# Attention output of a fused decoder layer carried by DMA transfers in token order, with new step orders on every engine

## What is computed

```python
x = x + attn(layernorm(x), W_qkv, W_out)            # causal, 16 heads of 16
x = x + mlstm(layernorm(x), ctx, ctx, gates, gain)  # 8 heads of 32
x = x + moe(layernorm(x), router, up, down)         # 8 experts, top 2

# the end of attn:
out = einsum('bnqk,bnkh->bnqh', softmax(scores), v)
out = out.reshape(B, -1, S)
return einsum('bds,nhd->bsd', out, W_out)
```

## Time and profile before

| | us |
|---|---|
| median of 3 runs | 968.09 |
| lowest, highest | 965.02, 971.19 |
| the profiled execution | 962.93 |
| its span, first to last instruction | 961.2 |
| TensorE busy | 887.1 |
| VectorE, ScalarE, GpSimd busy | 586.2, 487.4, 496.3 |

### The profile page before, as it was taken

One profiled execution on the slowest core, in us unless ns is written; L12 is line 12 of the kernel. 1 busy time (PEld: TensorE's weight loads), 2 busy tenths in 40 slices (PEclk: granted clock), 3 DMA queues, 4 the chain that ended last, 5 costly groups with the idle time before them and its releaser, 6 DMA issues.

```text
span 961.2 us, 31757 instructions
## 1 busy us (share of the span) xinstructions
PE 887.1 (92%) x11966; PEld 653.0 (68%) x11966; DVE 586.2 (61%) x1292; ACT 487.4 (51%) x839; POOL 496.3 (52%) x705
## 2 busy tenths in 40 slices
PE   5999999999997689899998988999999999999995
PEld 3667667667665356565564776778888888878783
DVE  4856766766764456777777657455555555555552
ACT  3667677677666367566455542333333333333331
POOL 2556666566565333366666667534444434444432
PEclk9999999999999799999888899999999999999998
DMA  9222443443445654455453233433332333233322
GB/s 283 70 57 67 93 129 90 96 127 90 92 119 121 172 183 132 146 177 179 144 162 118 90 86 89 87 62 51 48 51 47 53 49 52 46 52 52 47 34 23
DMA packets 133197, 92.96 MB, mean 97 GB/s; under 512 B 75712, under 2 KB 114112, under 8 KB 132928
## 3 DMA queue, kind: packets, MB, share of 16 engines
q1 hardware_dynamic: 119760, 73.10, 28.2%
q0 software_dynamic: 13296, 17.83, 11.1%
HBM read 54.65 MB, written 37.32 MB: 96 GB/s over the span
## 4 chain that ended last, share of the span: by engine, by line
PE 80%; DVE 7%; ACT 5%; issue 3%; DMA 2%; SPq 2%; another core or an unknown queue 1%; POOL 0%; DVEq 0%; ACTq 0%; POOLq 0%
PE pair L933 19%; PE pair L949 12%; PE pair L951 6%; PE pair L634 5%; PE pair L671 5%; PE pair L657 4%; PE pair L811 3%; PE pair L607 3%; PE pair L684 2%; PE pair L825 2%; PE pair L829 2%; PE pair L861 2%; PE pair L900 2%; PE pair L786 1%; PE pair L837 1%
## 5 line engine op out<-in xcount | busy, mean ns | idle before, releaser
L933 PE MATMUL pair<-XTs,WU 128*128 128x128 bf16 x3408 | 283.9, 219 | 5.9 <-DVE XTs L1269 2.9
L933 PEld LDWEIGHTS pair<-XTs,WU 128*128 x3408 | 238.1, 98 | 71.7 <-issue 8.7
L1603 POOL DMA_INDIRECT out_d<-XB x71 | 116.1, 1635 | 207.4 <-DVE XB L1291 174.0
L949 PE MATMUL pair<-WD,Hh 128*128 x568 | 214.8, 379 | 1.3 <-issue 1.3
L1469 ACT ACTIVATE Hf<-pair 128x512 f32<-128x512 f32 x142 | 84.8, 597 | 219.5 <-PE pair L933 207.9
L1282 DVE CAST Hh<-Hf 128x512 bf16<-128x512 f32 x142 | 64.5, 454 | 172.1 <-ACT Hf L1469 166.9
L951 PE MATMUL pair<-WD,Hl 128*128 x568 | 154.7, 272 | 0.0
L1284 DVE TENSOR_TENSOR Hl<-Hf,Hh 128x512 bf16<-128x512 f32 x142 | 99.5, 701 | 4.9
L1514 POOL TENSOR_SCALAR_AFFINE_SELECT PT<-PT 128x512 f32<-128x512 f32 (+1 forms) x96 | 73.9, 787 | 44.2 <-ACT PT L1320 28.7
L1576 POOL DMA_INDIRECT xs_scr<-XB,WGf x64 | 66.9, 1045 | 31.7 <-issue 18.2
L1488 POOL TENSOR_TENSOR LS<-LS,mhalf 128x2 f32<-128x2 f32 x48 | 34.1, 711 | 94.6 <-DVE LS L976 93.9
(11 more groups left out here) (243 smaller groups left out, 1728.9 us busy)
## 6 DMA issues: line engine op xcount, KB each, us to landing
XB<-xs_scr SPq DMA_DIRECT2D x71, 130.0 KB
STG<-wup_in SPq DMA_DIRECT2D x32, 256.0 KB
q_scr<-SPL SPq DMA_DIRECT2D x16, 512.0 KB, 4.2
STG<-wdn_in SPq DMA_DIRECT2D x32, 256.0 KB
o_scr<-On SPq DMA_DIRECT2D x32, 128.0 KB, 4.2
Mm<-o_scr SPq DMA_DIRECT2D x16, 256.0 KB, 3.0
CnT<-ctxt_in SPq DMA_DIRECT2D x16, 256.0 KB, 4.0
CX<-ctx_in SPq DMA_DIRECT2D x16, 256.0 KB, 4.4
```

The lines of the kernel that those rows point to most:

```text
L933: t = e.matmul(upb(j, k)[:, 128 * (fm % 4):128 * (fm % 4) + 128], WU[:, bass.ds(reg[j] * 4096 + off, 128)], XTs[:, r, hx, dk, :], start=n ...
L949: e.matmul(yb[r][:, 0:512], Hh[:, r, hsl], WD[:, bass.ds(reg[i] * 4096 + 512 * fk, 512)], start=fk == 0, stop=False, skip_group_check=True)
L1603: e.indirect_dma_start(out=out, out_offset=bass.IndirectOffsetOnAxis(ap=XS[:, i % NX, 256:257].bitcast(I32), axis=0), in_=Yf[:, i % NY, :] ...
```

## The change

- A4, its PSUM pair, On, Mm and the transposes of Mm go. ScalarE's copy to OTs now permutes the order within each partition.
- Step OT (SP) moves the row of denominators of each group of heads to `dnc`, 32 by 4 partitions, and stores OTs into `o_scr` in four transfers with runs of 64 floats, in the order of the tokens. XA (SP) reads it back with tokens in partitions. RC (VectorE) computes reciprocals times wsq, as 128x32. WB (SP) stores them with four transfers to the new scratch `r_scr`, BC (SP) reads them back, each row 16 times over, as XR with two transfers. X1 (VectorE) multiplies XA by XR and adds the product to x.
- The heads of Q and K are placed in another order in the weights, and PV picks V's columns accordingly.
- A6s, A6n and A6c run for batch b-3 instead of b-4 in a round, the query transposes in AX for b-3, the gate sums in MG for b-4 instead of b-5. `attention_rest` holds fewer steps.
- `ROUND` and `ORDER` have new orders on every engine. In attention SP loads the odd weight chunk of a round first and the even one after BC. ScalarE does A6c ahead of QK's copies. In the mLSTM TensorE does PV of part 2 and B5 between D of part 1 and D of part 2, and PV of part 0 at the end of the round; the two splits of a round on GpSimd no longer stand next to each other.

```diff
 ROUND = {
-    "tensor": "AX:1 MG:1 S1:0:0 T0:1:0 PV:2 S1:0:1 QK:-1 T0:1:1 S0:0 VX:0 T2:1 GT:15 weights:1:2 A4:2",
-    "vector": "Gp:16 weights:-2:0 A6s:4 weights:-1:1 S1:0:1 S0:0 VX:0 A4:2 weights:1:2 MG:0 AX:0 S1:-1:0 Gs:15 A0s:-3",
-    "scalar": "PV:2 A0n:-2 QK:-1 T0:1:1 Gt:13 A6c:4 weights:-2:0 A6n:4 VX:0 T2:1 weights:-1:1 AX:0 GT:15 MG:0 T0:0:0",
-    "gpsimd": "weights:0:2 split:0 T0:1:0 T0:1:1 split:0 GT:15 T2:1 A6c:4 A0s:-3 A6s:3",
-    "sync": "GT:15 load:0 A4:3 AX:1 Go:16 queries:16 decays:16",
+    "tensor": "MG:1 S1:0:0 T0:1:0 PV:2 S1:0:1 QK:-1 T0:1:1 S0:0 VX:0 T2:1 GT:15 weights:1:2 AX:0",
+    "vector": "A0s:-2 X1:3 S1:0:1 weights:-2:0 Gp:16 A6s:3 weights:-1:1 S0:0 weights:1:2 RC:2 Gs:15 MG:0 AX:0 S1:-1:0",
+    "scalar": "PV:2 A0n:-2 weights:-2:0 Gt:13 A6c:3 QK:-1 T0:1:1 VX:0 weights:-1:1 A6n:3 T2:1 AX:0 GT:15 MG:0 T0:0:0",
+    "gpsimd": "split:0 T0:1:0 A6s:3 T0:1:1 GT:15 weights:0:2 A6c:3 split:0 T2:1 A0s:-3",
+    "sync": "load:0:1 GT:15 BC:3 queries:16 load:0:0 AX:1 Go:16 OT:2 decays:16 XA:2 WB:2",
 }
 
-LIMITS = {"S1": (0, B - 1), "T0": (0, B - 1), "PV": (0, B - 2), "A0s": (0, B - 1), "A0n": (0, B - 1), "QK": (0, B - 1), "A6s": (0, B - 4),
-          "A6n": (0, B - 4), "S0": (0, B - 1), "VX": (0, B), "T2": (0, B - 1), "A6c": (0, B - 4), "A4": (0, B - 2), "AX": (-2, B), "MG": (0, B)}
+LIMITS = {"S1": (0, B - 1), "T0": (0, B - 1), "PV": (0, B - 2), "A0s": (0, B - 1), "A0n": (0, B - 1), "QK": (0, B - 1), "A6s": (0, B - 3),
+          "A6n": (0, B - 3), "S0": (0, B - 1), "VX": (0, B - 1), "T2": (0, B - 1), "A6c": (0, B - 3), "X1": (0, B - 3), "OT": (0, B - 2), "XA": (0, B - 2),
+          "RC": (0, B - 2), "WB": (0, B - 2), "BC": (0, B - 2), "AX": (-2, B), "MG": (0, B)}
 
...
             if kind == "load":
                 if ok(b):
-                    yield kind, 2 * b, 0
-                    yield kind, 2 * b + 1, 0
+                    yield kind, 2 * b + u, 0
             elif kind == "split":
                 if ok(b):
                     yield kind, parts, 0
...
                 yield kind, b, u
     yield "GE", 0, 0
     yield "PV", B - 1, 0
-    yield "MG", B + 1, 0
-    yield "A4", B - 1, 0
+    yield "OT", B - 1, 0
     yield "contexts", 0, 0
+    yield "queries", 1, 0
+    yield "WB", B - 1, 0
+    yield "XA", B - 1, 0
     yield "decays", 1, 0
-    yield "queries", 1, 0
     yield "contexts", 1, 0
...
-    return {(0, 0): (("A6s", z - 2), ("Mm", z), ("X1", z - 1), ("A6n", z - 2), ("A6c", z - 2)),
-            (0, 1): (("A6s", z - 1), ("XQ", z - 2), ("A6n", z - 1), ("A6c", z - 1)), (0, 2): (("X1", z), ("A6s", z)),
-            (1, 0): (("GA", z - 2), ("A6n", z)), (1, 1): (("XQ", z - 1), ("A6c", z)), (2, 0): (("XQ", z),), (2, 1): (("GA", z - 1),),
-            (3, 0): (("GA", z), ("Gt", 1)), (3, 1): (("GT", 1),), (3, 2): (("Gs", 1),), (4, 2): (("GE", 1),), (5, 0): (("Gp", 1),),
-            (5, 1): (("Go", 1),)}
+    return {(0, 0): (("RC", z), ("GA", z - 2), ("A6c", z - 1), ("X1", z - 1), ("A6n", z - 1), ("A6s", z - 1),), (0, 1): (("XQ", z - 1),),
+            (0, 2): (("X1", z), ("A6s", z),), (1, 0): (("GA", z - 1), ("A6n", z),), (1, 1): (("XQ", z), ("A6c", z),),
+            (2, 0): (("Gt", 1), ("GA", z),), (2, 1): (("GT", 1),), (2, 2): (("Gs", 1),), (3, 2): (("GE", 1),), (4, 0): (("Gp", 1),),
+            (6, 2): (("Go", 1),)}
 
...
 
 ORDER = {
-    "tensor": "D:0:0 B6:4 R4:5 PV:1:1 S:0:0 rest:0:0 D:0:1 PV:1:2 rest:0:1 D:0:2 B5:3 S:0:1 PV:0:0 rest:0:2 B4:1 S:0:2",
-    "vector": "B4x:2 rest:0:0 S:0:0 R5:5 R6:5 rest:0:1 B5s:2 S:0:1 rest:0:2 R2:4 B4:1 first:14 R3:4 S:0:2 R1:3",
-    "scalar": "rest:0:2 split:0 B4p:2 D:0:0 B5n:3 split:0 rest:0:0 D:0:1 rest:0:1 split:0 R1:4 B3:1 B5:3 D:0:2",
-    "gpsimd": "B4p:2 rest:0:0 sc:0 R6:5 split:0 split:0 sc:0 rest:0:1 sc:0 split:0 rest:0:2 B5s:2",
-    "sync": "load:0 rest:0:2 B1:0:1 B1:-1:0 rest:0:0 B4o:2 rest:0:1 row:15",
+    "tensor": "D:0:0 B6:4 R4:5 PV:1:1 rest:0:0 S:0:0 D:0:1 rest:0:1 PV:1:2 B5:3 D:0:2 S:0:1 rest:0:2 B4:1 S:0:2 PV:0:0",
+    "vector": "R5:5 R6:5 B4x:2 rest:0:0 S:0:0 rest:0:1 B5s:2 S:0:1 R2:4 rest:0:2 B4:1 R3:4 first:14 S:0:2 R1:3",
+    "scalar": "split:0 rest:0:2 B4p:2 D:0:0 split:0 R1:4 B5n:3 rest:0:0 D:0:1 rest:0:1 B3:1 split:0 B5:3 D:0:2",
+    "gpsimd": "split:0 B4p:2 sc:0 R6:5 split:0 rest:0:0 rest:0:2 sc:0 sc:0 split:0 rest:0:1 B5s:2",
+    "sync": "rest:0:2 rest:0:0 load:0 B1:0:1 B1:-1:0 B4o:2 row:15 rest:0:1",
 }
 
...
+    rsc = nc.dram_tensor("r_scr", (B, 16 * D), F32, kind="Internal").ap()
     qsc = nc.dram_tensor("q_scr", (B, 128, 2048), BF, kind="Internal").ap()
...
-        wsq = sb("wsq", [128, 2, NH], F32, ca)
-        On = sb("On", [128, 2, NH, 16], F32, ca)
-        Mm = sb("Mm", [128, 2, 2, 256], F32, ca)
+        dnc = sb("dnc", [128, 32], F32, ca)
+        rc = sb("rc", [128, 32], F32, ca)
+        wsq = sb("wsq", [128, 32], F32, ca)
+        XA = sb("XA", [128, 2, 2, 256], F32, ca)
+        XR = sb("XR", [128, 2, 256], F32, ca)
         QN = sb("QN", [128, 2, 256], F32, ca)
         CnT = sb("CnT", [128, 2, 256], F32, ca)
...
                         for par in range(2):
                             for kt in range(2):
                                 for j in range(4):
-                                    c = 17 * (8 * a + 2 * j + par)
+                                    c = 17 * (4 * j + 2 * a + par)
                                     if kt == 0:
                                         pt = blk(3 * b + a).rearrange("p (j r c) -> p j r c", j=4, r=2)[:, j, par, :]
...
                 elif kind == "VX":
...
-                    if ok(b - 3):
-                        m = b - 3
-                        w.wait_ge(l_m[m % 2], 16 * (m // 2 + 1))
...
-                            for tt in range(2):
-                                t = e.transpose(ps[:, 1, 256 * tt + 128 * dk:256 * tt + 128 * dk + 128], Mm[:, m % 2, dk, 128 * tt:128 * tt + 128], idf)
-                        t.then_inc(mT.sem, 1)
-                elif kind == "A4":
-                    pair_free(w, "A4", b)
-                    ps = pair_of("A4", b)
-                    w.wait_ge(ot_.sem, ot_.at(b))
-                    for tt in range(2):
-                        for g in range(4):
-                            o = ps[:, tt, 256 * (g // 2):256 * (g // 2) + 256].rearrange("p (j r c) -> p j r c", j=4, r=2)[:, :, g % 2, :]
-                            t = e.transpose(o, OTs[:, g, 128 * tt:128 * tt + 128], idf)
-                    t.then_inc(oT.sem, 1)
                 elif kind == "AX":
                     pair_free(w, "AX", b)
                     ps = pair_of("AX", b)
-                    for x_, m, src in ((1, b - 4, QN), (0, b + 2, xn)):
+                    for x_, m, src in ((1, b - 3, QN), (0, b + 2, xn)):
...
-                    if ok(b - 5):
-                        tensor_gate_sums(e, w, b - 5, ps[:, 1, 0:32])
+                    if ok(b - 4):
+                        tensor_gate_sums(e, w, b - 4, ps[:, 1, 0:32])
...
+        def vector_denominators(e, w, b):
+            w.wait_ge(l_dc, 16 * (b + 1))
+            w.wait_ge(l_wb, 64 * b)
+            e.reciprocal(dnc[:, :], dnc[:, :]).then_inc(dvc.sem, dvc.up())
+            w.wait_ge(dvc.sem, dvc.n)
+            e.tensor_tensor(rc[:, :], dnc[:, :], wsq[:, :], ALU.mult).then_inc(rc_.sem, 1)
+
+        def vector_residual(e, w, b):
+            r = b % 2
+            w.wait_ge(l_xa[r], 16 * (b // 2 + 1))
+            w.wait_ge(l_bc, 32 * (b + 1))
+            e.tensor_tensor(XA[:, r, :, :], XA[:, r, :, :], XR[:, :, :], ALU.mult).then_inc(dvc.sem, dvc.up())
+            w.wait_ge(dvc.sem, dvc.n)
+            e.tensor_tensor(xb(b), XA[:, r, :, :], xb(b), ALU.add).then_inc(x1_.sem, 1)
...
-                elif kind == "VX" and ok(b - 3):
-                    m = b - 3
-                    w.wait_ge(mT.sem, mT.at(m))
-                    e.tensor_tensor(xb(m), pair_of("VX", b)[:, 1, :].rearrange("p (t c) -> p t c", t=2), xb(m), ALU.add).then_inc(x1_.sem, 1)
-                elif kind == "A4":
-                    bv = pair_of("A4", b)[:, :, :].rearrange("p t (n c) -> p t n c", c=32)
-                    w.wait_ge(oT.sem, oT.at(b))
-                    w.wait_ge(l_o, 32 * b)
-                    e.reciprocal(bv[:, :, :, 16], bv[:, :, :, 16]).then_inc(dvc.sem, dvc.up())
-                    w.wait_ge(dvc.sem, dvc.n)
-                    e.tensor_tensor(rc[:, :, :], bv[:, :, :, 16], wsq[:, :, :], ALU.mult).then_inc(dvc.sem, dvc.up())
-                    w.wait_ge(dvc.sem, dvc.n)
-                    e.tensor_tensor(On[:, :, :, :].rearrange("p t n c -> p (t n) c"), bv[:, :, :, 0:16].rearrange("p t n c -> p (t n) c"),
-                                    rc[:, :, :].rearrange("p t (n a) -> p (t n) a", a=1).broadcast_to([128, 2 * NH, 16]),
-                                    ALU.mult).then_inc(on_.sem, 1)
+                elif kind == "RC":
+                    vector_denominators(e, w, b)
+                elif kind == "X1":
+                    vector_residual(e, w, b)
```

(54 more changed lines are left out.)

79 lines of the change are left out of this document (32 added, 47 removed).

## The result

The kernel after takes 963.03 us (median of 20 runs, 957.46 to 975.17); the kernel before, in as many runs beside it, 969.08 us. The ratio is 0.9935, 95% interval 0.9915 to 0.9956: 6.3 us faster, against the 17 us forecast. The profiled execution took 961.52 us (span 959.4), the one of before 962.93 (span 961.2). So the two traces differ by 1.8 us only, and single stages differ by far more than that.

The account below looks back on a forecast made before the run. TensorE was taken to bound attention, 95% busy. From 962.9 us profiled, 14.1 us off in attention, 0 in the handover and 3 in mLSTM gave 945.8, a ratio of 0.982, or 951 us on the median; range 938 to 974 us.

Parts of the forecast that it names:

- The floor: Steady attention round on TensorE: 18.11 us less 1.46 us of f32 transposes gives 16.65 us, the 0.73 us wait staying.
- 17.1 us: Average attention round, each the later of the X1 loop and TensorE's 16.65 us; over 14 rounds 14.1 us off.
- the X1 loop: Attention, S0 -> RC -> WB -> BC -> X1 -> S1: 16.0 us, 0.65 us of room; 16.6 us with collisions.
- The context loop: Attention, from S0 through RC, WB, BC's issues, context load, A6c and QK's copies to S0: 15.9 us, "as close".
- The forecast's own sign for a loop as the bound: In attention, TensorE idle before T0 or S0 until VectorE's Mp every round, or ScalarE idle before the context's copy.
- GpSimd and X1: VectorE's X1 blocked by GpSimd on the shared port: one collision, 1.2 us, in half the rounds, 0.6 us a round.
- rival C: Attention: both X1 instructions meet GpSimd every round, 18.1 us, the old period; 966 us in all; chance 0.21.
- B: Attention: TensorE stays the bound, transfers land early, GpSimd misses X1; rounds of 16.65 us, 940 us; chance 0.22.
- D: Attention: the X1 loop becomes the bound, WB landing in 4.2 us, 19.1 us a round; 986 us; chance 0.12.
- The handover: Attention to mLSTM: TensorE's 4.62 us stall goes, waits for RC and X1 come; 0, between -5 and +8 us.
- mLSTM: New orders in the mLSTM stage: -3 us, between -8 and +5.
- The sentence on D and exps: mLSTM: D of part 2 waited for ScalarE's exp in 13 rounds, 7.6 us; PV and B5 now stand between.

Follow-up runs that it names:

- the loop cut: Kernel after with SyncE's context load a round earlier (956.05 us), with ScalarE's A6c behind QK's copies (952.15 us), or with both (935.76 us, another kind of chip).
- The experiment with BC in four: BC in four issues of half the size instead of two, on the kernel with the copies first: 958.08 us, ratio 1.0176 to the kernel before.
- the kernel with the copies first: Kernel after with ScalarE's A6c moved behind QK's copies and T0's second pair of exps: 952.15 us, ratio 0.9809 to the kernel before.

## Why the prediction failed

**The direction and the bound.** TensorE was the bound of attention and the f32 transposes did leave it: 230.28 to 211.49 us busy. The floor was put at 16.65 us a round. It is 17.34 us, which most rounds reach once the loop is cut: the wait for xTl is 0.96 instead of 0.73 us, and one of 0.24 us for QN is new. That makes 17.1; the last 0.2 us is in no visible wait. By rounds of 17.34 the attention could gain some 10 us, not 14 or 20. With the loop cut, PV0 to PV13 is in fact 226.0 us, 5.9 less than before. The order of AX and MG was kept, as the forecast said, but A4's transposes had stood ahead of AX, and without them TensorE comes to QN before ScalarE has it.

**The step that failed** is the average, "17.1 us". It took the later of the X1 loop and TensorE's work. The context loop was in the text, summed at 15.9 us and called "as close", and then left out; and it was summed 2.5 us too short. Measured term by term in the round shown, and over the ten rounds from RC at 92.99 to RC at 276.12 us of the same trace:

| term of the context loop, us | forecast | round shown | mean of ten | from, to |
|---|---|---|---|---|
| RC | 0.6 | 0.98 | 0.96 | 0.89, 0.98 |
| WB, first issue to BC's first | 3.7 | 3.69 | 4.05 | 3.68, 4.91 |
| BC's issues | 0.9 | 1.29 | 1.29 | 1.28, 1.31 |
| chunk and queries' store, to CnT's issue | 0.9 | 2.43 | 1.34 | 1.01, 2.43 |
| context load, issue to A6c | 4.0 | 4.02 | 5.07 | 4.02, 6.32 |
| A6c, QK's copies, S0 and its reductions | 5.75 | 5.58 | 5.60 | 5.57, 5.70 |
| sum | 15.9 | 18.0 | 18.3 | 17.35, 19.57 |

The last term is 5.57 to 5.61 us in nine of the ten rounds: RC follows A6c at a fixed distance, so the loop closes in each of them (in the tenth, of 17.35 us, TensorE's own work is as long). Of the 2.5 us that the forecast lacks on average, 1.1 are the landing of the context load, 0.8 time in SyncE's queue (BC's issues and what stands behind them), and 0.35 each RC and WB, less 0.15 in the last term. Two other traces of the kernel after have the same terms: rounds of 18.4 and 18.5 us, the load at 5.3 and 5.2 us. The round shown, with 1.5 us in the queue and a landing of 4.0 us, is not the common one. Where the issues behind BC took 1.4 us and more, the load landed 4.0 to 4.4 us after its issue; where they took 1.0 us, 4.9 to 6.3 us after. From BC's last issue to A6c it is 5.7 to 7.4 us either way, against the forecast's 4.9. Whether the load would land sooner without the chunk and the store in front of it was not tested. A loop with no room takes each late landing at full length, which is why rounds of 19 to 21 us appear. The forecast's own sign for a loop as the bound, ScalarE idle before the context's copy, is in every one of these rounds.

**GpSimd and X1.** Sized at 0.6 us a round, with rival C at 2.1 us: measured in X1 0.14 us on average (L992 at 692 ns, L994 at 833 ns), and in RC's product nearly 0.4 us in almost every round, which the forecast had at the old 0.19 us. Together that is close to the 0.6 us, but not at the step that was named, and RC is in the context loop too. In the round shown X1 had begun first, and GpSimd was the one that lost. Two instructions of its own beside X1, against the same two without it:

```profile
175.00 1.23 POOL L1471 TENSOR_SCALAR LS<-LS 128x1 f32<-128x1 f32 x2
...
180.40 0.50 POOL L1471 TENSOR_SCALAR LS<-LS 128x1 f32<-128x1 f32 x2
```

The Trainium skill, "SBUF — State Buffer", Terms, has the loser of the shared port blocked; the trace agrees with it for both engines: GpSimd was the loser beside X1 (1.23 against 0.50 us), VectorE in RC's product, which began 0.09 us after GpSimd's cast (0.58 against 0.19 us).

**The X1 loop.** WB 3.7 us and BC 3.7 us from its first issue to X1 (forecast 3.7 and 3.9): right to 0.2 us in the round shown and in most others. X1 waits 0.57 us for XR there. The experiment with BC in four shows that this loop had about 1 us of room, and bears out its sum. By "DMA: Bandwidth & Descriptors", Rules for kernel authors, of the Trainium skill BC would have been at its high end, 4.4 us with the second issue; the time was 3.7 us, and on how many DMA engines BC ran no row shows.

**The rivals.** C's time, 966 us, is nearest of the rivals, and its sign for the attention is right (the gain is eaten, rounds of 18), but its mechanism, collisions with GpSimd, is not. B fell: its rounds of 16.65 us are below what TensorE reaches in a steady round of any of these kernels with the loop cut. D named the right kind of thing, a loop through SyncE's queue as the bound, with the wrong branch; on chips of 939 us the change is indeed no gain (1.003).

**The handover** was taken as 0, between -5 and +8. From PV15 to the first add it is -1.7 and -0.6 us in the two pairs, as said. But the two rounds ahead of PV15 cost 5 us, which no term held: MT comes 0.9 us later (3.30 against 2.4 us of idle), the gate scans Gs now stand ahead of VectorE's AX and hold PV14 by 1.7 us more, and PV14 runs mostly at the lower clock.

**mLSTM**, -3 us, between -8 and +5, measured -9.0 and -9.8, just outside. The sentence on D and exps saw one wait. What the runs show is more: the orders of VectorE and GpSimd (adds off the collisions among them), TensorE's order by itself, and either only together with the rest of the change.

So 14.1 + 0 + 3 became -3.2 - 5.3 + 1.7 + 9.0 in the first pair of traces; with 0.3 earlier at the start and 0.7 later in the experts that is the 1.8 us between the spans. The medians say 6 us. That the kernel came out faster at all, and within the stated range, is luck: attention and its last rounds lost 8.4 us where 14 were to be gained, and the mLSTM orders, forecast at 3 us, gained three times that. What of the difference between one pair of executions and the medians belongs to which stage stays open.

## What to carry to other kernels

Where one queue issues for several chains, write the loop through each of them with every issue that stands between and with the spread of each landing, not one value, and give the period the longest of all; a sum called "as close" is a second bound, not a remark. A load whose buffer is free goes ahead of an issue that waits, and an engine's step that waits for a transfer goes behind those that wait for nothing: the one was worth 8 and the other 12 us on the chip of 969 us, where the kernel with the copies first is at 0.981 of before. On the other kind of chip both together bring it from 1.003 to 0.9945. New orders of steps belong to the handover they were made for and are measured together with it.

## What the runs showed of the hardware

The same kernel takes 963 to 969 us on two chips and 939 to 940 us on two others. The steady rounds of attention with the loop cut are alike on both kinds to 0.01 us (17.34 and 17.35). What differs is the mLSTM stage, where two batches in the middle take 24.1 to 24.6 us in the kernel after on the one kind and 21.7 to 21.9 us on the other, with a granted clock of 1.00 from 420 to 500 us on both (in the first trace of the kernel after TensorE is busy for 18.8 to 19.1 of every 20 us there, on the chip of 939 us for 20.0), and what follows the last add, 408 to 412 against 403 to 405 us. No run shows why. The change is a gain on the one kind (0.9935 and 0.9962) and none on the other (1.0030); the kernel before has no trace on the second kind, so which stage makes that difference stays open.

One issue on SyncE's queue of the same 512 KB store took between 0.33 and 1.79 us, with nothing in the profile that it waited for.

The same 256 KB context load was waited for between 3.6 and 6.3 us after its issue in attention (ScalarE's step idle until it landed each time).
